# The causal mask of the maxima's scores: 26 rows inside the score products in place of a mask product for each tile

## What is computed

```python
h = concatenate([tokens_of_image(x), txt], axis=1)       # colour matrix, curve, clip: 256 tokens + 128 of text
scores = einsum("bqhd,bkhd->bhqk", q, k) * scale         # q, k, v from layernorm(h)
scores = where(tril(ones((t, t))), scores, -inf)
probs = softmax(scores, axis=-1)
h = h + (einsum("bhqk,bkhd->bqhd", probs, v).reshape(b, t, d) @ W_O)
h = h + top2_of_8_experts(layernorm(h)) + bias           # gelu feed-forward, capacity 384 tokens per expert
```

## Time and profile before

| | us |
|---|---|
| median of 3 runs | 658.73 |
| lowest and highest of them | 657.36, 666.75 |
| the profiled execution | 664.39 |
| its span, first to last instruction | 662.7 |
| mean granted clock of TensorE in it | 0.979 of full |

### The profile page before, as it was taken

How to read it: one execution, slowest core, us unless ns; L and a number is a source line. 1 busy time by engine, 2 the same in 40 slices (tenths; PEclk the granted TensorE clock), 3 DMA queues, 4 the chain that set the end, 5 groups by cost and what they waited for, 6 DMA issues and landing times.

```text
span 662.7 us, 13744 instructions
## 1 busy us (share of the span) xinstructions
PE 608.2 (92%) x5082; PEld 508.2 (77%) x5082; DVE 399.6 (60%) x950; ACT 377.1 (57%) x818; POOL 388.4 (59%) x602
## 2 busy tenths in 40 slices
PE   1788999999999999999878899999999999999992
PEld 1465666676767666666558899999999999999992
DVE  5789788788998888678464333334554555344320
ACT  4448786777777785765641554445454454545540
POOL 4303233424556555556556499998877777888223
PEclk9979999999999999999899799999999999999997
DMA  6437676633534232371012825454444434442113
GB/s 231 124 80 179 196 203 179 182 102 99 145 98 113 72 104 82 105 221 36 34 48 63 285 93 110 115 112 112 112 110 81 97 82 105 112 109 45 20 23 38
DMA packets 66604, 73.86 MB, mean 111 GB/s; under 512 B 6312, under 2 KB 61586, under 8 KB 66536
## 3 DMA queue, kind: packets, MB, share of 16 engines
q1 hardware_dynamic: 56232, 59.45, 30.3%
q0 software_dynamic: 9504, 13.00, 11.5%
q10 hardware_dynamic: 800, 0.52, 0.3%
HBM read 31.62 MB, written 22.48 MB: 82 GB/s over the span
## 4 chain that ended last, share of the span: by engine, by line
PE 80%; ACT 5%; issue 5%; DVE 3%; DMA 2%; SPq 1%; POOL 1%; ACTq 0%; DVEq 0%; POOLq 0%
PE t_bank L1790 20%; PE bank L1805 14%; PE s_bank L1805 7%; PE bank L695 7%; PE t_bank L660 5%; PE s_bank L638 5%; PE t_bank L754 3%; PE s_bank L639 2%; PE t_bank L723 2%; PE s_bank L1775 1%; PE t_bank L738 1%; PE t_bank L760 1%; PE bank L707 1%; DVE g L1235 1%; ACT part L1032 1%
## 5 line engine op out<-in xcount | busy, mean ns | idle before, releaser
L1752 DVE TENSOR_TENSOR hl<-h,hh 128x384 fp32r<-128x384 f32 x128 | 102.9, 809 | 157.9 <-ACT h L1715 157.9
L553 POOL TENSOR_SCALAR_AFFINE_SELECT pt<-pt 128x256 f32<-128x256 f32 x192 | 82.0, 433 | 150.2 <-ACT pt L973 116.7
L1192 DVE TENSOR_REDUCE mx<-s_bank 128x2 f32<-128x256 f32 (+2 forms) x192 | 122.9, 683 | 34.2 <-PE s_bank L639 33.7
L1712 ACT ACTIVATE hh<-t_bank 128x384 fp32r<-128x384 f32 x128 | 63.0, 492 | 135.0 <-PE t_bank L1790 132.7
L1665 POOL DMA_INDIRECT out<-yo,xr x48 | 74.8, 1558 | 59.1 <-ACT yo L1723 48.9
L973 ACT ACTIVATE pt<-t_bank 128x512 f32<-128x512 f32 x128 | 76.1, 602 | 30.6 <-PE t_bank L660 29.4
L1652 POOL TENSOR_TENSOR wl<-wr,wh 128x256 fp32r<-128x256 f32 x112 | 92.5, 859 | 1.2
L1790 PE MATMUL t_bank<-xh,wh 128*128 128x384 f32 x256 | 87.1, 340 | 0.6 <-DVE xl L1746 0.6
L1790 PE MATMUL t_bank<-xl,wh 128*128 128x384 f32 x256 | 86.5, 338 | 0.0
L1790 PE MATMUL t_bank<-xh,wl 128*128 128x384 f32 x256 | 86.4, 338 | 0.0
L638 PE MATMUL s_bank<-ks,qs 96*128 96x128 bf16 (+2 forms) x384 | 80.0, 278 | 1.6 <-DMA ks<-part 1.5
(11 more groups left out here) (205 smaller groups left out, 1341.4 us busy)
## 6 DMA issues: line engine op xcount, KB each, us to landing
wr<-in_w SPq DMA_DIRECT2D x16, 1024.0 KB, 5.8
qs<-part SPq DMA_DIRECT2D x96, 96.0 KB
ks<-part SPq DMA_DIRECT2D x90, 96.0 KB
slot_rows<-empty SPq DMA_DIRECT2D x4, 1560.0 KB, 9.4
xr<-slot_rows SPq DMA_DIRECT2D x16, 390.0 KB, 3.3
wr<-in_x SPq DMA_DIRECT2D x8, 768.0 KB, 5.5
out<-hid SPq DMA_DIRECT2D x8, 384.0 KB, 6.2
qs<-mT ACTq DMA_DIRECT2D x64, 3.0 KB
```

What stands on the lines that cost most here:

```text
L553: pool.affine_select(out=blocks, in_=blocks, compare_op=ALU.is_ge, fill=0.0, base=0, pattern=[[0, 2], [1, P]], channel_multiplier=-1).then ...
L1192: ins = dve.tensor_reduce(mx[:, p // 2, j, 2 * (p % 2):2 * (p % 2) + 2], pair_region(s_bank, j), AX_X, ALU.max)
L1752: dve.tensor_tensor(hl[:, f, :], h[f % 2][:, :], hh[:, f, :].bitcast(F32), ALU.subtract).then_inc(hl_done, 1)
```

## The change

The mask product goes. In its place the stacks have 128 rows instead of 98, and rows 98 to 123 (26 of them) hold a pattern whose product over queries and keys of one 128 x 128 tile is hugely negative above the diagonal and nearly nothing elsewhere. Each row serves five neighbouring queries (`GROUP`), with powers of two 26 binary places apart. A tile's scores now come from two products: the keys before the tile's own 128, over rows 0 to 95 (absent for j = 0), and the tile's own 128 over all 128 rows. For that product rows 96 and 97 of `qs` must be zero while the maxima are sought, so SP clears them, by a transfer of two rows from `qs[0][0]`, ahead of each half's query stack from the third sequence on (12 transfers). The pattern is made by POOL at the start of its program (3 memsets and 11 selects on 32 rows), spread over the 24 tiles of `ks[0][0]` and `qs[0][0]` by two copies of DVE at the start of its program, and sent to the other six stacks by SP.

```diff
@@
 SLOTS = TOPK * E * CAP
 EPS = 1e-5
 SCALE = 1.0 / np.sqrt(HD)
-MASKED = -1.0e30
+GROUP = 5
+STEP_UP = 26
+LEAST = 4
 
 
 Q_PARTS = (0, 0, 0, 1, 1, 2)
@@
 MROW = len(Q_PARTS) * HD
 MPARTS = 2
 SROWS = MROW + MPARTS
+EDGE = P - MROW
 GH = 4
 BANK_TILES = ((0, 2), (1,))
 NW = KC * FFN
@@
+def edge(i):
+
+    return 2.0 ** (STEP_UP * i - STEP_UP * GROUP // 2)
+
+
 def rows_to_all(ap, n):
 
     return bass.AP(tensor=ap.tensor, offset=ap.offset, ap=[[0, P], [1, n]])
@@
     hid = buf("hid", [P, B, NT, DIM])
     ident_b = buf("ident_b", [P, P], BF16)
     minus_b = buf("minus_b", [P, P], BF16)
-    mask_q = buf("mask_q", [P, P], BF16)
+    edge_k = buf("edge_k", [P, P], BF16)
+    edge_q = buf("edge_q", [P, P], BF16)
     eps_t = buf("eps_t", [P, NT])
     neg_half = buf("neg_half", [P, NT])
     flag_f = buf("flag_f", [1, 2])
@@
-    less = buf("less", [P, MPARTS * HALF * T // P], BF16)
@@
 
 
 
-    qs = [[lent(f"qs{q}{h}", [SROWS, HALF, T], BF16) for h in range(2)] for q in range(2)]
-    ks = [[lent(f"ks{q}{h}", [SROWS, HALF, T], BF16) for h in range(2)] for q in range(2)]
+    qs = [[lent(f"qs{q}{h}", [P, HALF, T], BF16) for h in range(2)] for q in range(2)]
+    ks = [[lent(f"ks{q}{h}", [P, HALF, T], BF16) for h in range(2)] for q in range(2)]
@@
     consts = sem("consts")
     masks = sem("masks")
     ones_made = sem("ones_made")
-    minus_made = sem("minus_made")
-    minus_in = sem("minus_in")
+    edge_step = sem("edge_step")
+    edge_rows = sem("edge_rows")
+    edge_in = [sem(f"edge_in{i}") for i in range(3)]
+    cleared = [sem(f"cleared{h}") for h in range(2)]
@@
         queue.wait_ge(*part_made(b, k, stage))
         if b >= 2 and stage == 0:
             queue.wait_ge(t_ready, 12 * (2 * (b - 2) + half + 1))
+            if s == 0:
+                queue.dma_start(dst[MROW:SROWS, :, :], qs[0][0][P - MPARTS:P, :, :]).then_inc(cleared[half], 16)
         for at, piece in enumerate(K_PARTS if s else Q_PARTS):
             if piece == stage:
                 queue.dma_start(dst[at:MROW:len(Q_PARTS)], part[k][stage][:, :]).then_inc(landed or stack_in[half], 16)
@@
         load_x(1)
         sp.dma_start(mat[:, MAT_WO:NMAT], mats[:, MAT_WO:NMAT]).then_inc(rest_in, 16)
         sp.dma_start(hid[:, 1:B, NT - 1, :], txt[1:B].rearrange("b p d -> p b d")).then_inc(text_in[1], 16)
-        sp.wait_ge(minus_made, 1)
-        for q in range(2):
-            for h in range(2):
-                sp.dma_start(ks[q][h][MROW:SROWS, :, :].rearrange("r h t -> r (h t)"), less[:, :]).then_inc(minus_in, 16)
+        sp.wait_ge(edge_rows, 2)
+        for i, (q, h) in enumerate(((0, 1), (1, 0), (1, 1))):
+            for of in (ks, qs):
+                sp.dma_start(of[q][h][MROW:P, :, :], of[0][0][MROW:P, :, :]).then_inc(edge_in[i], 16)
         load_x(2)
         for i in range(3):
             stack(sp, 0, 0, i)
@@
                 empty_rows(n)
 
     def gpsimd(pool):
+        of_k, of_q = edge_k[MROW:P, :], edge_q[MROW:P, :]
+        pool.memset(of_k, -edge(GROUP)).then_inc(edge_step, 1)
+        pool.memset(of_q, 0.0).then_inc(edge_step, 1)
+        for i in range(GROUP):
+            at = GROUP - 1 - i
+            pool.wait_ge(edge_step, 2 * i + 2)
+            pool.affine_select(out=of_k, in_=of_k, compare_op=ALU.is_ge, fill=-edge(at), base=GROUP * MPARTS - at - 1,
+                               pattern=[[1, P]], channel_multiplier=-GROUP).then_inc(edge_step, 1)
+            pool.affine_select(out=of_q, in_=of_q, compare_op=ALU.not_equal, fill=2.0 ** -LEAST / edge(at),
+                               base=GROUP * MPARTS - at, pattern=[[1, P]],
+                               channel_multiplier=-GROUP).then_inc(edge_step, 1)
+        pool.wait_ge(edge_step, 2 * GROUP + 2)
+        pool.affine_select(out=of_k, in_=of_k, compare_op=ALU.is_ge, fill=0.0, base=GROUP * MPARTS,
+                           pattern=[[1, P]], channel_multiplier=-GROUP).then_inc(edge_step, 1)
+        pool.wait_ge(edge_step, 2 * GROUP + 3)
+        pool.memset(edge_k[MROW:SROWS, :], -1.0).then_inc(edge_step, 1)
+        pool.wait_ge(edge_step, 2 * GROUP + 4)
+
         pool.memset(ident[:, :], 0.0).then_inc(consts, 1)
         pool.memset(eps_t[:, :], EPS).then_inc(consts, 1)
         pool.memset(neg_half[:, :], -0.5).then_inc(consts, 1)
@@
                            pattern=[[-1, P]], channel_multiplier=1).then_inc(consts, 1)
         pool.wait_ge(consts, 4)
         pool.tensor_copy(ident_b[:, :], ident[:, :]).then_inc(consts, 1)
-        pool.memset(less[:, :], -1.0).then_inc(minus_made, 1)
         pool.memset(minus_b[:, :], 0.0).then_inc(masks, 1)
-        pool.memset(mask_q[:, :], 0.0).then_inc(masks, 1)
-        pool.wait_ge(masks, 2)
+        pool.wait_ge(masks, 1)
         pool.affine_select(out=minus_b[:, :], in_=minus_b[:, :], compare_op=ALU.not_equal, fill=-1.0, base=0,
-                           pattern=[[-1, P]], channel_multiplier=1).then_inc(masks, 1)
-        pool.affine_select(out=mask_q[:, :], in_=mask_q[:, :], compare_op=ALU.is_ge, fill=MASKED, base=0,
                            pattern=[[-1, P]], channel_multiplier=1).then_inc(masks, 1)
 
         pool.wait_ge(prm_in, 16)
@@
             m = 4 * n + p
             if p == 0 and grp == 0:
                 pe.wait_ge(stack_in[half], stack_count(b, half))
-                if n == 0:
+                if b >= 2:
+                    pe.wait_ge(cleared[half], 16 * (b - 1))
+                elif n:
+                    pe.wait_ge(edge_in[n - 1], 16 * 2)
+                else:
+                    pe.wait_ge(edge_rows, 2)
                     pe.wait_ge(stack_soft, 16 * len(K_PARTS))
             if m == 0 and grp == 0:
                 for i in range(3):
@@
                 h = 2 * p + i
                 for j in BANK_TILES[grp]:
                     dst, w = s_region(s_bank, j, i)
-                    pe.matmul(dst, q[0:MROW, h, j * P:(j + 1) * P], k[0:MROW, h, 0:w], start=True, stop=False)
-                    mm = pe.matmul(dst[:, j * P:(j + 1) * P], ident_b[:, :], mask_q[:, :], start=False, stop=True)
+                    own = slice(j * P, w)
+                    if j:
+                        pe.matmul(dst[:, 0:j * P], q[0:MROW, h, own], k[0:MROW, h, 0:j * P], start=True, stop=True)
+                    mm = pe.matmul(dst[:, own], q[:, h, own], k[:, h, own], start=True, stop=True)
             mm.then_inc(s_ready, 1)
 
         def shifted_scores(n, p, unit):
@@
                 pe.wait_ge(m_in[p // 2], 16 * MPARTS * (n + 1))
                 if n == 0 and p == 0:
                     pe.wait_ge(ones_made, 2)
-                    pe.wait_ge(minus_in, 16 * 4)
             if at < 2:
                 release(f"t{at}")
             else:
@@
             for h, j, col in (((2 * p, 0, 0), (2 * p, 2, T)), ((2 * p, 1, 0), (2 * p + 1, 1, 2 * P)),
                               ((2 * p + 1, 0, 0), (2 * p + 1, 2, T)))[unit]:
                 w = T - j * P
-                mm = pe.matmul(bank[:, col:col + w], k[:, h, j * P:(j + 1) * P], q[:, h, j * P:T], start=True, stop=True)
+                mm = pe.matmul(bank[:, col:col + w], k[0:SROWS, h, j * P:(j + 1) * P], q[0:SROWS, h, j * P:T],
+                               start=True, stop=True)
             mm.then_inc(t_ready, 1)
 
         def maxima(n, grp):
@@
                 pe.matmul(t_bank[:, 1, 0:P], ident_b[:, :], ident_b[:, :], start=True, stop=True)
 
         pe.wait_ge(consts, 5)
-        pe.wait_ge(masks, 4)
+        pe.wait_ge(masks, 2)
         pe.wait_ge(relu_done, CH)
         turning(56)
         for c in range(KC):
@@
                               bias.rearrange("p (o d) -> p o d", o=1).to_broadcast([P, NT, DIM]),
                               ALU.add).then_inc(res_last, 1)
 
+        dve.wait_ge(edge_step, 2 * GROUP + 4)
+        for dst, edge_of in ((ks, edge_k), (qs, edge_q)):
+            dve.tensor_copy(dst[0][0][MROW:P, :, :].rearrange("r h (j c) -> r (h j) c", c=P),
+                            edge_of[MROW:P, :].rearrange("r (o c) -> r o c", o=1)
+                            .to_broadcast([EDGE, HALF * NT, P])).then_inc(edge_rows, 1)
         dve.wait_ge(prm_in, 16)
         dve.tensor_reduce(flag_f[:, 0:1], slope_t[0:1, :].rearrange("p (c n) -> p c n", c=CH)[:, :, 1:PTS],
                           mybir.AxisListType.XY, ALU.max, apply_absolute_value=True).then_inc(passed, 1)
```

## The result

Twenty runs of each: 659.79 us before (657.09 to 666.75), 655.17 after (652.73 to 656.79); ratio 0.9917 with a 95% interval from 0.9894 to 0.994. By the ratio that is 5.5 us off, 0.8%, by the medians 4.6, where 12.6 were forecast, and the median lies 0.2 us above the predicted range. The profiled execution of the changed kernel has a span of 653.4 us against 662.7, at a mean clock of 0.980 against 0.979.

A forecast was written before the change was run, and what follows sets the result against it. The prediction took PE to bound attention: of 22.5 us removed there 14.2 would arrive, less 1.6 for the start, so -12.6 us from the median of 658.73 to 646.1 us, with a range of 637 to 655 us (8 in 10).

The forecast's parts named there:

- What bounds the kernel: Attention: PE sets the pace, busy 36.9 of 37.8 us per middle period; DVE has 4.5 us of room, ACT 9.4.
- What goes: 384 mask products leave PE, priced by columns at 0.057 us per 128 (0.11 at the lower clock): 22.5 us.
- What of it arrives: Attention: of 22.5 us saved on PE, 14.2 shorten the run; 1.9 per middle period, 9.5 for five.
- sign of being wrong: Middle of attention: a period staying above 36.8 us, meaning DVE or ACT bound, would show the prediction wrong.
- The first sequence: Attention up to 60 us, DVE nearly the bound: 1.4 us gained, the stretch at the lower clock included.
- The start: Before the first colour product: DVE waits for POOL's pattern and copies it twice, 1.6 us later, arriving whole.
- rival 3: Start: the copies run element by element, costing 4.0 us; 10.2 us off in all, 648.5 us; chance 0.07.
- Clears, constants, transfers: SP's 12 clears, POOL's later constants and SP's six pattern transfers are covered by slack and cost nothing.
- Rival 2: Attention: DVE becomes the bound and a third of the saving arrives, 7.5 us; 652.8 us; chance 0.20.
- Rival 1: Attention: almost all the saving arrives because PE's waits don't grow, 22.5 us; 637.8 us; chance 0.17.
- rival 4: Split diagonal products each cost a mask product more than their columns, so 7.9 us come off PE; 655.3 us; chance 0.05.
- Rival 5: Attention: with less to do PE is granted 1.2 GHz; at a mean clock of 0.90, 668.7 us; chance 0.03.

The follow-up runs named there:

- b_dve: Kernel before, DVE's image instructions of sequences 2 to 7 cut from 512 to 32 elements per partition: 667.05 us, ratio 1.0000.
- b_exp: Kernel before, ACT's exponentials of sequences 2 to 7 cut to a quarter: 662.14 us, ratio 0.9916.
- b_all: Kernel before, sequences 2 to 7: DVE's and ACT's image instructions cut from 512 to 32 elements, ACT's exponentials to a quarter; 654.24 us, ratio 0.9826.
- a_max: Changed kernel, sequences 2 to 7: DVE's and ACT's image work cut to 32 elements, exponentials to a quarter, maxima to 32 columns; 636.78 us, ratio 0.9657.
- b_max: Kernel before, sequences 2 to 7: DVE's and ACT's image work cut to 32 elements, exponentials to a quarter, maxima to 32 columns; 647.18 us, ratio 0.9814.
- a_exp: Changed kernel, ACT's exponentials of sequences 2 to 7 cut to a quarter: 658.30 us, ratio 0.9871.
- b_nomask: Kernel before, its 384 mask products left out and nothing put in their place: 661.13 us, ratio 0.9925.
- a_noclear: Changed kernel without SP's twelve clears: 661.89 us, ratio 0.9942.
- a_moved: Changed kernel, DVE's two copies moved into two later pauses and SP's six transfers behind the third image's load: 663.46 us, ratio 0.9966.

## Why the prediction was wrong

**What bounds the kernel.** PE, but not alone: b_dve's ratio is 1.000, b_exp's 0.9916. "DVE has 37.8 - 33.3 = 4.5 us per period, ACT 9.4" was read as room. b_all shows how much of PE's 37.7 was its own: at most 36.3. The kernel before already lost 1.4 us per pair to answers of the other two, and PE's busy 36.9 hid most of it: for the same products b_all shows 35.9 us busy.

**What goes.** Right: 0.057 us per 128 columns, 640 products, clock 1.00 in the middle. At the limit, a_max against b_max, 1.94 us of the 2.7 per period come off, so "nothing" for the split and the rest was too little by 0.8 us a period. The split's own part of that is small: start to start, a tile of 384 keys took 0.165 us and takes 0.112 + 0.057 now, some 0.1 us a period with the tiles of 256.

**What of it arrives: the step that failed.** "That leaves 1.9 us per period, 9.5 us for five, and DVE would be 33.3 of 35.9 busy, which it can still be." It couldn't. The five periods gave 3.7 us, 0.74 each, and a period is 37.26 us, past the 36.8 that the prediction itself set as its sign of being wrong. The forecast counted the waits that the trace already showed, for `part` and `ckvT`, and let them grow by 0.8 us; these two grew by 0.2 us a period. What it left out was a wait that the trace of before doesn't show in these periods: `project` on xn and hid behind DVE's run of maxima, which the mask product ahead of it had covered. And the waits on the exponentials, which it put at 0.1 us a period because ACT had "28.4 us of work in 35.9", set the odd turns. DVE's idle 4.5 us lie where DVE waits for scores, not where PE waits for DVE.

**The first sequence** lost 0.9 us in these two profiles instead of gaining 1.4. With the lower clock in the same place there is a gain: turn 0 takes 14.22 us with the lower clock from 39.6 to 46.4 us, where b_exp has 15.40 (39.9 to 46.7); it takes 13.13 in a_exp (39.8 to 43.2), where b_max has 13.76 (39.4 to 42.8); and turn 1 takes 16.74 against 17.07 at the full clock. What eats the gain is where the lower clock falls, in turn 0 and in most profiles in turn 1 too, and the forecast had no term for that. b_nomask, with nothing added at the start, has the same; why it falls there is open.

**The start.** Worked out +1.6, measured +0.96 at the first colour product and +1.27 at the first scores. The sequence of steps up to the colours was right, the copies were mis-sized: 1.3 us each by bytes, 0.94 and 1.04 measured. "This arrives whole" isn't borne out: the +0.96 (0.4 to 1.0 against the eight profiles with the old start) is -0.35 at the end of the colour products and +0.55 at PE's first product on xn, since DVE's overlap with POOL moved. The +1.27 is mostly scatter: ten kernels with the changed start have their first scores at 34.5 to 35.7 us, eight with the old one at 33.9 to 35.0, means 0.4 us apart. The tier table in "VectorE: DVE Perf Modes" of the Trainium skill, by which the estimate was 0.96 us, was the better price; rival 3 is out.

**Clears, constants, transfers: nothing.** Right for the clears, by a_noclear: its turns are the changed kernel's to 0.01 us in the middle, and its ratio is no better. For the constants and transfers, the chain of waits up to the first scores has no piece of either beyond the pattern. That the cover exists where the steps were left, a_moved shows from the other side: moved, the same six transfers cost 2.6 us of PE's wait.

**The rivals.** Rival 2, a third arrives, was nearest: 652.8 us, where 5.5 us off 658.73 would be 653.2. Its mechanism was half of it: DVE bounds every second turn, ACT the others. Rival 1 is refuted by the turns, rival 4 by the spacing of the products. Rival 5 is refuted for the middle, where the clock is 1.00; the first sequence has something of it.

## What to carry to other kernels

Idle time of a second engine is no reserve until you know where it lies. When you take work off the bounding engine, look for each place where another engine's result arrives just in time, and ask what covered it: here the removed products were that cover, and of 10.9 us over eight turns 2.4 arrived, while 5.3 turned into waits for the two others. Price it by a kernel with the work simply left out: b_nomask would have told the ceiling, 5 us, before anything was built. And a limit that alternates between two engines isn't found by relieving one; cut both, then each alone.

## What the runs showed of the hardware

Two bf16 copies of DVE within SBUF, 3072 elements in each of 32 rows, took 0.94 and 1.04 us: some three elements per ns. While they ran, POOL was slowed: a memset of 128 x 3 took 0.92 us and the select behind it 0.81 us. a_moved is the control: the same two instructions, started at 5.50 and 5.79 us with no copy beside them, took 0.11 and 0.29 us. No piece of this stands in the chain of waits to the first scores, but a large copy on DVE isn't free for POOL.

It goes the other way too. DVE's product over two tensors of 512 f32 takes 0.74 us in most of its 48 runs in the kernel before, and 1.09 and 1.75 us in the two that ran beside POOL's cast and two-tensor product on `up_h` and `up_l`. In the changed kernel, where POOL's two come later, none of the first six takes over 0.76 us, and it is the curve product beside `up_l` that takes 1.57 us.
